# The last expert layer in pairs of slots with whole-batch rings, its loads and first gathers during the selection

## The chip, the cores and the metric

The kernel runs on one core of a Trainium2 chip. Time is device time in microseconds (us). The core's engines are TensorE (PE; its weight loads are shown as PEld), VectorE (DVE), ScalarE (ACT), GpSimd (POOL) and SyncE (SP). SyncE issues plain DMAs, GpSimd the indirect ones (gathers by an index per partition); 16 DMA engines carry both. Engines run their own instruction streams and meet at semaphores.

## The reference

x has the shape (8, 2048, 256) in float32: 8 batches of 2048 tokens. Three steps are added to it in turn:

```
x = x + 0.5 * ffn(layernorm(x));  x = x + attn(layernorm(x));  x = x + 0.5 * ffn(layernorm(x))
ffn(x):  gates  = sinkhorn(x @ gate_w)                  # (b, 2048, 8 experts), 8 iterations
         vals, idx = top_k(gates over the tokens, 256)  # per batch and expert
         out[e]    = x[idx[e]] @ experts[e] * vals[e]   # 256 tokens x 256, experts are 256 x 256
         result    = zeros(b, 2048, 256); result[idx] = out   # .set: of several experts on one token one wins
attn(x): a projection, a short convolution, a selective scan over 2048 steps with 16 states, a gate, a projection
```

## The kernel before

The program runs five stages, each with instruction streams of its own and a barrier of all engines behind it: constants; `route` "in" (gates and selection for the first ffn); `mixer` (the first ffn's experts and all of attn); `route` "mid" (L137 to L150: gates and selection for the second ffn); `ffn` (L1445 on: its experts and the final sum). The change is in the last two.

`route` has two halves. `gates_stage` loads all rows, normalises them, stores them to `normed_rows` in HBM and makes the gates. `top_stage` (L451 on) finds the 256 largest gates of each of 64 rows (batch, expert): VectorE does 32 rounds of MAX8, FIND_INDEX8 and MATCH_REPLACE8, merges two half rows by a bitonic exchange, and turns the result into tables. `slot_token` says for each slot of a batch which token it takes (a slot is 128 of the 256 places of one expert, so a batch has SL = 16 slots), `slot_gate` its gates, and `token_row`, which comes last, from which row of the results each token takes its own. For `token_row` VectorE builds 16 comparison tables (L603), which TensorE multiplies (L645).

`ffn` works by slots, and VectorE, GpSimd and SyncE have their streams unrolled over NB + 2 turns of a batch; TensorE and ScalarE do batch 0 written out and the others in a loop. For slot s of batch b:

- GpSimd gathers 128 tokens' rows into `f_picked` (L1532, "gather out"), after the turn of the slot 8 before;
- TensorE turns them (two transposes, L1606), one slot ahead of the products; VectorE copies the result from PSUM (L1570); TensorE multiplies by the expert's weights (L1613); ScalarE scales by the gate into `f_routed` (L1593); SyncE stores that to `routed_rows` (L1506).
- The way back: once all 16 stores of batch m have landed (and `token_row` is copied, L1562), GpSimd gathers for each of the 16 token tiles t the rows from `routed_rows` into `f_back` (L1544, "gather back"), VectorE adds them to `f_total`, which holds the batch's x (L1579), and SyncE stores the 2 MB when all 16 are added (L1513).

Every ring (`f_picked`, `f_routed`, `f_back`) has 8 buffers. The order is written out: in turn (b, s) GpSimd issues first the gather out of slot s and then the gather back that is BRING = 22 slots behind; VectorE does the copy of slot s and then the addition that is JOIN = 26 slots behind. So gather back t waits for the addition of t - 8, and that one stands in VectorE's order behind the copy of the slot four before the one that GpSimd is at:

```
pool.wait_ge(added, count(m * T + t - NK + 1))
```

The experts' 2 MB and the first two batches of x (2 MB each) are loaded by SyncE at the start of `ffn`; the loads of later batches go out between its stores.

Of the kernel before, what the change touches and what calls it, by code (L numbers as in the profile page):

```python
# [27 lines left out]
P = 128  # L28
NB = 8
# [9 lines left out]
YR = E * (M + 1)  # L39
ITERS = 8  # L40
# [96 lines left out]
def route(nc, g, x, tag):  # L137
# [3 lines left out]
    with ExitStack() as ctx:  # L141
        held = nc.snapshot_sems()
        rows = ctx.enter_context(nc.sbuf_tensor(f"gate_rows_{tag}", [P, NT // 2], F32))
        with ExitStack() as c1:
            gates_stage(nc, g, x_in, xn_out, rows, tag, c1)
        with ExitStack() as c1:
            top_stage(nc, g, rows, tag, c1)

        nc.clear_and_free_semaphores(nc.allocated_since(held))
        nc.all_engine_barrier()  # L150
# [300 lines left out]
def top_stage(nc, g, rows, tag, ctx):  # L451
# [40 lines left out]
    part_built, part_used, merged = sem("part_built"), sem("part_used"), sem("merged")  # L492
    ps_mirror = ctx.enter_context(nc.psum_tensor(f"ps_mirror_{tag}", [P, 2 * M], F32))
    FINAL = (M.bit_length() - 1) % 2
    block = ctx.enter_context(nc.Block())

    @block.gpsimd
    def _(pool):
        nc.gpsimd.memset(mirror[:], 0.0).then_inc(mirror_made, 1)
        pool.wait_ge(mirror_made, 1)  # L500
        nc.gpsimd.affine_select(out=mirror[:], in_=mirror[:], compare_op=ALU.not_equal, fill=1.0,
                                base=1 - P, pattern=[[1, P]], channel_multiplier=1).then_inc(mirror_made, 1)

    @block.vector
    def _(dve):
# [71 lines left out]
        def step(ins):  # L577
# [5 lines left out]
        dve.wait_ge(tok_copied, 1)  # L583
        flat = token_f[:].rearrange("p r h -> p (r h)")
# [5 lines left out]
        nc.vector.tensor_tensor(g.slot_token[:], token_f[:].rearrange("p (b e) h -> p b (e h)", b=NB),  # L590
                                g.token_base[:].unsqueeze(2).to_broadcast([P, NB, SL]), ALU.add)
# [853 lines left out]
def ffn(nc, g, x, out, ctx):  # L1445
# [11 lines left out]
    NX = NY = NK = 8  # L1457
    NT4 = 4
    BRING, JOIN, LOAD = SL + 6, SL + 10, 3
    expert = sb("f_expert", [P, E, KD, D])  # L1460
    slot_now = [sb(f"f_slot_now{i}", [P, SL], I32) for i in range(2)]
    row_now = [sb(f"f_row_now{i}", [P, T], I32) for i in range(2)]
    picked = [sb(f"f_picked{i}", [P, D]) for i in range(NX)]
    picked_t = [sb(f"f_picked_t{i}", [P, KD, P]) for i in range(NT4)]
    routed = [sb(f"f_routed{i}", [P, D]) for i in range(NY)]
    back = [sb(f"f_back{i}", [P, D]) for i in range(NK)]
    total = [sb(f"f_total{i}", [P, T, D]) for i in range(2)]
    ps_turn = [ps(f"f_ps_turn{i}") for i in range(NT4)]
    ps_out = [ps(f"f_ps_out{i}") for i in range(NT4)]
    expert_in, now_set, rows_set = sem("f_expert_in"), sem("f_now_set"), sem("f_rows_set")  # L1470
    picked_in = [sem(f"f_picked_in{i}") for i in range(NX)]
    routed_out = [sem(f"f_routed_out{i}") for i in range(NY)]
    back_in = [sem(f"f_back_in{i}") for i in range(NK)]
    x_in = [sem(f"f_x_in{i}") for i in range(2)]
    out_stored = [sem(f"f_out_stored{i}") for i in range(2)]
# [15 lines left out]
    def behind(b, s, lag):  # L1491

        k = (lag - s + SL - 1) // SL
        return b - k, s - lag + SL * k

    @block.sync
    def _(sp):
        def load_x(b):
            sp.dma_start(total[b % 2][:], x_v[b]).then_inc(x_in[b % 2], 16)

        def turn(b):
            for s in range(SL):
                e, h = s // NH, s % NH
                if there(b):
                    sp.wait_ge(scaled, b * SL + s + 1)
                    sp.dma_start(routed_v[b][e, 1 + h * P:1 + (h + 1) * P, :],  # L1506
                                 routed[s % NY][:]).then_inc(routed_out[s % NY], 16)
                if s == LOAD and there(b - 1) and there(b - 3):
                    sp.wait_ge(out_stored[(b - 1) % 2], (b - 1) // 2 * 16)
                    load_x(b - 1)  # L1510
                if s == JOIN - SL + 2 and there(b - 2):
                    sp.wait_ge(added, (b - 1) * T)
                    sp.dma_start(out_v[b - 2], total[b % 2][:]).then_inc(out_stored[b % 2], 16)  # L1513

        for e in range(E):
            sp.dma_start(expert[:, e, :, :], g.experts[e].rearrange("(k p) f -> p k f", p=P)).then_inc(expert_in, 16)
        load_x(0)
        load_x(1)
        rounds(turn)
        for odd in range(2):  # L1520
            sp.wait_ge(out_stored[odd], NB // 2 * 16)

    @block.gpsimd
    def _(pool):
        def turn(b):
            for s in range(SL):
                if there(b):
                    if s == 0:
                        pool.wait_ge(now_set, b + 1)
                    pool.wait_ge(turned, count(b * SL + s - NX + 1))  # L1530
                    pool.sem_inc(g.passed_pool, 1)
                    nc.gpsimd.indirect_dma_start(  # L1532
                        out=picked[s % NX][:], out_offset=None, in_=g.normed,
                        in_offset=bass.IndirectOffsetOnAxis(ap=slot_now[b % 2][:, s:s + 1].bitcast(U32), axis=0)
                    ).then_inc(picked_in[s % NX], 16)
                m, t = behind(b, s, BRING)
                if there(m):
                    if t == 0:
                        pool.wait_ge(rows_set, m + 1)
                        for k in range(NY):  # L1540
# [131 lines left out]
```

## Time and profile before

| | us |
|---|---|
| median of 3 runs (lowest, highest) | 3817.17 (3815.45, 3819.61) |
| the profiled execution | 3821.82 |
| its span, first to last instruction | 3820.3 |
| second selection (`top_stage` "mid") | about 3228 to 3413 |
| `ffn` | about 3413 to 3820 |
| mean granted TensorE clock | 0.856 |

A row of the timeline is: start, duration (us from the span's start), engine, line, operation, output<-inputs, sizes, count if alike instructions were merged, and in brackets the idle time of the engine before it and what ended it. "issue" means that the engine waited for nothing that the profile shows, "remote" that it waited for something that the profile can't name. An ending "q" (SPq) is an engine's queue: there the duration is from first to last issue. DMA-issuing instructions of GpSimd have durations of their own (DMA_INDIRECT); the data lands later. TensorE's ends are modelled. The clock is the granted share of full speed; its two levels are 0.5 (1.2 GHz) and 1.0 (2.4 GHz).

### The profile page before, as it was taken

The numbers are of one execution on the slowest core, as the hardware profiler recorded it, in microseconds if no ns is written. First come the engines' busy times: TensorE is split into PE (matmuls) and PEld (weight loads), VectorE is DVE, ScalarE is ACT, GpSimd is POOL, SyncE is SP. The second block draws the span as 40 slices with busy tenths as digits, with TensorE's granted clock in tenths as the row PEclk, the third lists the DMA queues.
The fourth block names the chain that finished last, engine by engine and source line by source line (L and its number), as shares of the span: only waits on it lengthen the run. The fifth ranks groups of instructions, "written<-read, shape, count | busy, mean of one in ns | idle before, by whom it ended". The sixth has DMA issues, their size and how long they took to land. (4 is left out here: it accounts for less than half of the span.)

```text
span 3820.3 us, 29742 instructions
## 1 busy us (share of the span) xinstructions
PE 2787.8 (73%) x9244; PEld 1524.3 (40%) x9244; DVE 3107.9 (81%) x2624; ACT 2135.3 (56%) x2286; POOL 1281.8 (34%) x900
## 2 busy tenths in 40 slices
PE   8701488899799889889989979997896695025553
PEld 4501233345345445434534634543442454014442
DVE  5798059999999999999999999989999467972222
ACT  6300366876876787688687687678766262001111
POOL 0000247245344443624624434440110100015665
PEclk9655799999999999999989999999998896557776
DMA  6200448778778868867877787886775471024666
GB/s 260 111 0 11 127 113 178 156 162 165 177 171 170 179 147 177 186 145 165 183 161 172 157 177 168 173 175 121 144 139 121 80 286 67 0 92 136 216 217 240
DMA packets 146762, 575.75 MB, mean 151 GB/s; under 512 B 22160, under 2 KB 73936, under 8 KB 99792
## 3 DMA queue, kind: packets, MB, share of 16 engines
q0 software_dynamic: 77568, 402.71, 50.9%
q1 hardware_dynamic: 69072, 171.59, 12.2%
q8 instruction: 55, 0.90, 0.1%
q14 instruction: 67, 0.55, 0.0%
HBM read 154.72 MB, written 117.51 MB: 71 GB/s over the span
## 5 line engine op out<-in xcount | busy, mean ns | idle before, releaser
L1057 DVE TENSOR_TENSOR_SCAN state<-state,drive 128x2048 f32<-128x2048 f32 x512 | 2220.8, 4405 | 75.7 <-ACT state L1222 75.7
L1222 ACT ACTIVATE state<-delta,neg_a 128x2048 f32<-128x2048 f32 x512 | 1020.2, 2003 | 276.1 <-DMA state<-state 186.2
L1393 PE MATMUL ps_states<-state,ident 128*128 128x512 f32 x1800 | 898.5, 646 | 167.6 <-DMA state<-state 167.6
L953 POOL DMA_DIRECT2D state<-state x256 | 232.8, 911 | 1288.9 <-DVE state L1057 1264.3
L1393 PEld LDWEIGHTS ps_states<-state,ident 128*128 128x128 f32 x1800 | 363.9, 209 | 608.4 <-issue 399.1
L1329 PE MATMUL ps_proj<-x1t,w_in 128*128 128x512 f32 x1024 | 502.5, 627 | 77.9 <-ACT conv_in L1138 59.2
L1345 PE MATMUL ps_proj<-conv_in,tap 128*128 128x512 f32 x1024 | 456.9, 594 | 0.5 <-ACT conv_in L1138 0.5
L901 POOL DMA_INDIRECT picked<-normed_rows,slot_now x128 | 368.7, 2880 | 256.0 <-DVE gate_now L995 188.8
L917 POOL DMA_INDIRECT x<-routed_rows,row_now x128 | 334.7, 2615 | 154.5 <-issue 64.3
L1329 PEld LDWEIGHTS ps_proj<-x1t,w_in 128*128 128x128 f32 x1024 | 196.1, 197 | 345.5 <-issue 235.8
L1345 PEld LDWEIGHTS ps_proj<-conv_in,tap 128*128 128x128 f32 x1024 | 191.7, 189 | 245.4 <-issue 244.7
L1570 DVE COPY f_picked_t<-f_ps_turn 128x256 f32<-128x256 f32 x128 | 54.0, 424 | 278.7 <-remote 140.3
L1613 PE MATMUL f_ps_out<-f_expert,f_picked_t 128*128 128x256 f32 x512 | 183.3, 495 | 97.6 <-DVE f_picked_t L1570 53.7
L1593 ACT ACTIVATE f_routed<-f_ps_out,slot_gate 128x256 f32<-128x256 f32 x128 | 60.5, 474 | 339.9 <-remote 139.5
L1361 PE MATMUL ps_rows<-w_out,xc 128*128 128x256 f32 x768 | 204.8, 391 | 5.0 <-DVE xc L1036 5.0
L1532 POOL DMA_INDIRECT f_picked<-normed_rows,f_slot_now x128 | 121.7, 951 | 229.4 <-DVE f_slot_now L1556 185.8
L1361 PEld LDWEIGHTS ps_rows<-w_out,xc 128*128 128x128 f32 x768 | 188.4, 306 | 19.2 <-issue 8.3
L1145 ACT COPY delta<-ps_proj 128x512 f32<-128x512 f32 x128 | 73.8, 582 | 177.4 <-PE ps_proj L1345 177.3
L1613 PEld LDWEIGHTS f_ps_out<-f_expert,f_picked_t 128*128 128x128 f32 x512 | 116.4, 251 | 123.5 <-DVE f_picked_t L1570 59.4
L1544 POOL DMA_INDIRECT f_back<-routed_rows,f_row_now x128 | 122.3, 955 | 108.6 <-issue 46.0
L1302 PE MATMUL ps_rows<-expert,picked_t 128*128 128x256 f32 x448 | 118.5, 388 | 17.5 <-ACT picked_t L1103 17.5
L1324 PE MATMUL ps_rows<-ident,x 128*128 128x128 f32 x256 | 46.2, 328 | 108.8 <-ACT x L1124 81.3
(267 smaller groups left out, 3177.1 us busy)
## 6 DMA issues: line engine op xcount, KB each, us to landing
state<-state POOLq DMA_DIRECT2D x256, 1024.0 KB, 7.7
delta<-xc POOLq DMA_DIRECT2D x24, 1024.0 KB, 12.3
normed_rows<-rows_in SPq DMA_DIRECT2D x8, 2048.0 KB, 7.5
expert<-in_experts SPq DMA_DIRECT2D x64, 256.0 KB
routed_rows<-routed SPq DMA_DIRECT2D x128, 128.0 KB
x<-in_x POOLq DMA_DIRECT2D x16, 1024.0 KB, 10.6
x_rows<-x SPq DMA_DIRECT2D x16, 1024.0 KB, 7.8
x_rows<-rows_out POOLq DMA_DIRECT2D x64, 256.0 KB, 8.6
```

The source lines that it names most:

```text
L901: nc.gpsimd.indirect_dma_start(out=picked[s % NX][:], out_offset=None, in_=g.normed, in_offset=bass.IndirectOffsetOnAxis(ap=slot_now[:, s: ...
L917: nc.gpsimd.indirect_dma_start(out=x1[:, t, :], out_offset=None, in_=g.routed[0], in_offset=bass.IndirectOffsetOnAxis(ap=row_now[:, t:t + ...
L953: nc.gpsimd.dma_start(out=state[held(q)][:], in_=state[held(q - 1)][:], accum_op=ALU.add).then_inc(pair_landed(b, q // 2)[0], 16)
L1057: nc.vector.tensor_tensor_scan(state[held(q)][:], state[held(q)][:], drive[j % 2][:], 0.0, ALU.mult, ALU.add).then_inc(state_ready, 1)
L1222: nc.scalar.activation(state[held(q)][:], delta[j % 2][:], ACT.Exp, scale=g.neg_a[:, j, n:n + 1]).then_inc(decay_ready, 1)
L1329: mm = nc.tensor.matmul(ps_proj[bank][:], g.w_in[:, k, col:col + P], x1t[:, k, c * CH:(c + 1) * CH], start=(k == 0), stop=(k == KD - 1))
L1345: mm = nc.tensor.matmul(ps_proj[c % 2][:], tap[:, j * KC + k, :], conv_in[:, c * CH + k:c * CH + k + CH], start=(k == 0), stop=(k == KC - 1))
L1361: mm = nc.tensor.matmul(out_bank(r, last)[:, (t % 2) * D:(t % 2 + 1) * D], y_now[j].rearrange("p (n t) -> p n t", t=T)[:, :, t], g.w_out[: ...
L1393: mm = nc.tensor.matmul(ps_sum[c][:], g.ident[:], state[held(q)][:, c * CH:(c + 1) * CH], start=(opening and n == 1), stop=(n == N - 1))
L1532: nc.gpsimd.indirect_dma_start(out=picked[s % NX][:], out_offset=None, in_=g.normed, in_offset=bass.IndirectOffsetOnAxis(ap=slot_now[b % 2 ...
L1544: nc.gpsimd.indirect_dma_start(out=back[t % NK][:], out_offset=None, in_=g.routed[m], in_offset=bass.IndirectOffsetOnAxis(ap=row_now[m % 2 ...
L1613: mm = nc.tensor.matmul(ps_out[s % NT4][:, 0:D], picked_t[s % NT4][:, k, :], expert[:, s // NH, k, :], start=(k == 0), stop=(k == KD - 1))
```

## The change

In `route` "mid", between the gates and the selection, the buffers of the last layer are laid out: the experts, six buffers of x (`f_total`, NTOTAL = 6, before: 2) and a ring of eight pairs of `f_picked`. During the selection SyncE loads the experts and six batches of x, and GpSimd issues the 16 gathers out of batch 0, as soon as `slot_token` is set; that addition is moved ahead of five small conversions.

In `ffn` all work on slots is by pairs (the two slots of one expert): one wait, one copy of 512 columns, one addition of 512 columns and one store of 256 KB for two; gathers, transposes, products and scalings stay as many as before. The rings of `f_picked`, `f_routed` and `f_back` hold 8 pairs, which is a whole batch. The gather back is BRING = 11 pairs (22 slots) behind as before, the addition JOIN = 13 pairs (26 slots). The order inside a turn is gather out x2, gather back x2. Batches 6 and 7 of x are loaded, and all outputs stored, in four pieces (PIECES) of 512 KB.

The diff, cut to its core:

```diff
+NTOTAL = 6
+PIECES = 4
 def route(nc, g, x, tag, ctx):
+    if tag == "mid":
+        g.f_expert = ctx.enter_context(nc.sbuf_tensor("f_expert", [P, E, KD, D], F32))
+        g.total = [... f"f_total{i}", [P, T, D] ... for i in range(NTOTAL)]
+        g.picked = [... f"f_picked{i}", [P, 2, D] ... for i in range(SL // 2)]
     with ExitStack() as c1:
         top_stage(nc, g, rows, tag, c1)
 def top_stage(nc, g, rows, tag, ctx):
+    @block.sync
+    def _(sp):
+        if tag == "mid":
+            for e in range(E):
+                sp.dma_start(g.f_expert[:, e, :, :], g.experts[e].rearrange(...)).then_inc(g.f_expert_in, 16)
+            for b in range(NTOTAL):
+                sp.dma_start(g.total[b][:], x_v[b]).then_inc(g.total_in[b], 16)
     @block.gpsimd
+        if tag == "mid":
+            pool.wait_ge(slots_set, 1)
+            for s in range(SL):
+                nc.gpsimd.indirect_dma_start(
+                    out=g.picked[s // 2][:, s % 2, :], out_offset=None, in_=g.normed,
+                    in_offset=bass.IndirectOffsetOnAxis(ap=g.slot_token[:, 0, s:s + 1].bitcast(U32), axis=0)
+                ).then_inc(g.picked_in[s // 2], 16)
     @block.vector
         dve.wait_ge(tok_copied, 1)
+        nc.vector.tensor_tensor(g.slot_token[:], token_f..., g.token_base..., ALU.add).then_inc(slots_set, 1)
         (five conversions)
-        nc.vector.tensor_tensor(g.slot_token[:], token_f..., g.token_base..., ALU.add)
 def ffn(nc, g, x, out, ctx):
-    NX = NY = NK = 8
-    BRING, JOIN, LOAD = SL + 6, SL + 10, 3
+    NP = SL // 2
+    NR = NP
+    BRING, JOIN = NP + 3, NP + 5
+    TP = T // PIECES
  SyncE:
+        def store_out(m, i):
+            sp.wait_ge(added, m * NP + (i + 1) * TP // 2)
+            sp.dma_start(out_v[m, :, i * TP:(i + 1) * TP, :], total[m % NTOTAL][...]).then_inc(out_stored[m % NTOTAL], 16)
+            for p in range(NP):
+                    sp.wait_ge(scaled, 2 * (b * NP + p + 1))
+                    sp.dma_start(routed_v[b][p, 1:1 + M, :].rearrange("(h q) d -> q h d", h=NH), routed[p][:])...
+                m, t = behind(b, p, JOIN + 3)
+                if there(m) and t % 2 == 0: store_out(m, t // 2)
+                old = b - 3
+                if p % 2 and there(old) and there(old + NTOTAL):
+                    sp.wait_ge(out_stored[old], PIECES * 16)
+                    load_x(old + NTOTAL, p // 2)
  GpSimd:
+            for p in range(NP):
+                if 1 <= b < NB:
+                    if p == 0: pool.wait_ge(now_set, b)
+                    pool.wait_ge(turned, count(b * NP + p - NR + 1))
+                    for h in range(2): (gather out of slot 2p + h)
+                m, t = behind(b, p, BRING)
+                if there(m):
+                    if t == 0:
+                        pool.wait_ge(rows_set, m + 1)
+                        for k in range(NR): pool.wait_ge(routed_out[k], (m + 1) * 16)
+                    pool.wait_ge(added, count(m * NP + t - NR + 1))
+                    for h in range(2): (gather back of tile 2t + h)
  VectorE:
+                    dve.wait_ge(turned, b * NP + p + 1)
+                    dve.wait_ge(product, count(b * NP + p - NT4 + 1))
+                    nc.vector.tensor_copy(picked_t[p % NT4][...], ps_turn[p % NT4][:]).then_inc(copied, 1)
+                    dve.wait_ge(back_in[t], (m + 1) * 32)
+                    nc.vector.tensor_tensor(total[m % NTOTAL][:, 2 * t:2 * t + 2, :], ..., back[t][:], ALU.add).then_inc(added, 1)
  TensorE: (4 transposes of pair p, then 8 matmul instructions of pair p - 1)
+            pe.wait_ge(picked_in[p], (b + 1) * 32)
+            pe.wait_ge(copied, b * NP + p + 1)
  ScalarE:
+                act.wait_ge(product, b * NP + p + 1)
+                act.wait_ge(routed_out[p], b * 16)
+                for h in range(2): (scale slot 2p + h)
```

## Rows read from the trace of the kernel before

**Rows 1.** Windows: length; busy of PE, PEld, DVE, ACT, POOL; clock; DMA share; GB/s.
```profile
3228.00:3413.00 185.00, 9.85 (x144) 7.44 (x144) 174.71 (x284) 0.62 (x2) 0.50 (x2) 0.50 0.00 0
...
3454.00:3785.00 331.00, 186.66 (x655) 137.96 (x653) 82.55 (x229) 52.08 (x111) 205.33 (x216) 0.72 0.61 196
```

**Rows 2.** Timeline of GpSimd in the last layer: gathers at its start and end.
```profile
3453.99 0.94 POOL L1544 DMA_INDIRECT f_back<-routed_rows,f_row_now  x1 [5.79 <-PE f_ps_turn L1606]
3455.24 0.94 POOL L1532 DMA_INDIRECT f_picked<-normed_rows,f_slot_now  x1 [0.30 <-issue]
...
3790.64 1.18 POOL L1544 DMA_INDIRECT f_back<-routed_rows,f_row_now  x1 [4.26 <-DVE f_total L1579]
...
3810.26 0.95 POOL L1544 DMA_INDIRECT f_back<-routed_rows,f_row_now  x1 [0.30 <-issue]
```

**Rows 3.** Waits of GpSimd, 3454 to 3785: total us, times, longest.
```profile
POOL f_back L1544 <- issue: 41.0, 83, 5.2
POOL f_back L1544 <- DVE f_total L1579: 40.0, 20, 5.1
```

**Rows 4.** Timeline of all engines, end of one stop in the last layer.
```profile
3529.60 0.47 ACT L1593 ACTIVATE f_routed<-f_ps_out,slot_gate 128x256 f32<-128x256 f32 x1 [6.81 <-remote]
...
3532.33 0.42 DVE L1570 COPY f_picked_t<-f_ps_turn 128x256 f32<-128x256 f32 x1 [8.49 <-remote]
...
3532.80 2.08 PE L1613 MATMUL f_ps_out<-f_expert,f_picked_t 128*128 128x256 f32 x4 [6.94 <-issue]
...
3533.87 0.94 POOL L1544 DMA_INDIRECT f_back<-routed_rows,f_row_now  x1 [3.29 <-remote]
```

**Rows 5.** Windows at the start of the last layer, columns as in rows 1.
```profile
3425.00:3429.00 4.00, 4.00 (x13) 3.07 (x14) 0.55 (x2) 0.52 (x2) 2.83 (x3) 0.53 1.01 416
3429.00:3437.00 8.00, 6.18 (x33) 4.59 (x32) 2.03 (x5) 2.70 (x6) 4.21 (x5) 1.00 1.00 398
```

**Rows 6.** Timeline of VectorE at the end of the second selection.
```profile
3384.22 0.29 DVE L590 TENSOR_TENSOR slot_token<-token_f_mid,token_base 128x128 int32<-128x128 f32 x1
3384.43 2.28 DVE L593 TENSOR_TENSOR at_tile_mid<-tile_f_mid,iota_col 128x2048 bf16<-128x2048 f32 x1
...
3389.07 18.25 DVE L603 TENSOR_TENSOR at_part_mid<-part_f_mid,iota_col 128x1024 bf16<-128x1024 f32 x16
...
3412.27 0.23 DVE L613 CAST token_row<-won_mid 128x128 int32<-128x128 f32 x1
```

**Rows 7.** Timeline of VectorE and GpSimd in the middle stage.
```profile
1036.75 17.36 DVE L1057 TENSOR_TENSOR_SCAN state<-state,drive 128x2048 f32<-128x2048 f32 x4
...
1043.75 2.60 POOL L901 DMA_INDIRECT picked<-normed_rows,slot_now  x1 [0.30 <-issue]
...
1051.58 3.41 POOL L901 DMA_INDIRECT picked<-normed_rows,slot_now  x1 [0.30 <-issue]
```

**Rows 8.** Instructions of line 901: durations in ns, minimum, median, maximum.
```profile
L901 POOL DMA_INDIRECT picked<-normed_rows,slot_now x128: 940/3402/4335, 375.1 to 2428.9; - x128
```

**Rows 9.** Timeline of TensorE in the last layer: its start, and two turns at full clock.
```profile
3421.34 0.69 PE L1606 MATMUL f_ps_turn<-ident,f_picked 128*128 128x128 f32 x2 [13.57 <-DMA f_picked<-normed_rows,f_slot_now]
...
3454.43 0.38 PE L1606 MATMUL f_ps_turn<-ident,f_picked 128*128 128x128 f32 x2
...
3455.52 0.38 PE L1606 MATMUL f_ps_turn<-ident,f_picked 128*128 128x128 f32 x2
```

**Rows 10.** Timeline: last slot of batch 5, gathered and scaled; last slot of batch 7, gathered.
```profile
3677.09 0.95 POOL L1532 DMA_INDIRECT f_picked<-normed_rows,f_slot_now  x1 [0.30 <-issue]
...
3692.49 0.47 ACT L1593 ACTIVATE f_routed<-f_ps_out,slot_gate 128x256 f32<-128x256 f32 x1 [4.57 <-remote]
...
3774.09 0.94 POOL L1532 DMA_INDIRECT f_picked<-normed_rows,f_slot_now  x1 [0.30 <-DVE f_total L1579]
```

**Rows 11.** Timeline: the last store.
```profile
3813.52 0.34 SPq L1513 DMA_DIRECT2D out<-f_total  x1
```

**Rows 12.** Waits of ScalarE over the last layer, 3413 to 3821.
```profile
ACT f_routed L1593 <- remote: 139.5, 31, 8.8
```

More of the change, by code:

```diff
@@ L1501, in turn @@
         def turn(b):
-            for s in range(SL):
-                e, h = s // NH, s % NH
+            for p in range(NP):
                 if there(b):
[L1505 to L1518, printed above, removed]
+                    sp.wait_ge(scaled, 2 * (b * NP + p + 1))
+                    sp.dma_start(routed_v[b][p, 1:1 + M, :].rearrange("(h q) d -> q h d", h=NH),
+                                 routed[p ][:]).then_inc(routed_out[p ], 16)
+                m, t = behind(b, p, JOIN + 3)
+                if there(m) and t % 2 == 0:
+                    store_out(m, t // 2)
@@ L1597, in _, with turn @@
+        pairs(0)
         with act.Fori(1, NB) as b:
[L1598 removed]
+            pairs(b)
     @block.tensor
     def _(pe):
[L1602 to L1604 removed]
+        def turn(b, p):
+            pe.wait_ge(picked_in[p], (b + 1) * 32)
+            pe.wait_ge(copied, count(b * NP + p - NT4 + 1))
             for k in range(KD):
[L1606 removed]
+                for h in range(2):
+                    c = k * 2 + h
+                    mm = nc.tensor.transpose(ps_turn[p % NT4][:, c * P:(c + 1) * P], picked[p ][:, h, k * P:(k + 1) * P],
+                                             g.ident[:])
@@ L1607, in turn @@
             mm.then_inc(turned, 1)
-        def apply_expert(b, s):
-            pe.wait_ge(copied, b * SL + s + 1)
-            pe.wait_ge(scaled, count(b * SL + s - NT4 + 1))
-            for k in range(KD):
-                mm = nc.tensor.matmul(ps_out[s % NT4][:, 0:D], picked_t[s % NT4][:, k, :], expert[:, s // NH, k, :],
-                                      start=(k == 0), stop=(k == KD - 1))
-            mm.then_inc(product, 1)
-        def slots(b):
-            for s in range(SL + 1):
-                if s < SL:
-                    turn(b, s)
-                if s == 1 and isinstance(b, int):
-                    pe.wait_ge(expert_in, E * 16)
-                if s:
-                    apply_expert(b, s - 1)
@@ L1626, in _, with apply_expert, pairs @@
-        slots(0)
+        def apply_expert(b, p):
+            pe.wait_ge(copied, b * NP + p + 1)
+            pe.wait_ge(scaled, count(2 * (b * NP + p - NT4 + 1)))
+            for h in range(2):
+                for k in range(KD):
+                    mm = nc.tensor.matmul(ps_out[p % NT4][:, h * D:(h + 1) * D], picked_t[p % NT4][:, k, h, :], expert[:, p, k, :],
+                                          start=(k == 0), stop=(k == KD - 1))
+            mm.then_inc(product, 1)
+        def pairs(b):
+            for p in range(NP + 1):
+                if p < NP:
+                    turn(b, p)
+                if p == 1 and isinstance(b, int):
+                    pe.wait_ge(g.f_expert_in, E * 16)
+                if p:
+                    apply_expert(b, p - 1)
@@ L1627, in _ @@
+        pairs(0)
         with pe.Fori(1, NB) as b:
-            slots(b)
+            pairs(b)
 def program(nc, w, g):
```

155 lines of the change are left out of this document (75 added, 80 removed).

## The prediction, before the run

> **What bounds the kernel now.** I read stage windows first, then GpSimd's waits, then the order in time of the last stage. The windows show a second selection (3228 to 3413 us) in which VectorE is busy 174.7 of 185 us, GpSimd 0.5 us and the DMA share is 0.00, and then the last expert layer, in which no engine is full: from 3454 to 3785 TensorE is busy 187 of 331 us at a granted clock of 0.72, VectorE 83, ScalarE 52, GpSimd 205, DMA 0.61 [rows 1]. What the layer does throughout is issue gathers on GpSimd, 256 of them. One takes 0.94 us, and the next starts 1.25 us after it where nothing holds it (3453.99, 3455.24) [rows 2]. From the first gather back (3453.99) to the last (3810.26) there are 232 steps in 356.3 us; at 1.25 us they would be 290.0, so 66.3 us are stalls. The waits name them: gathers back wait 40.0 us for additions (20 times, up to 5.1 us) and 41.0 us with no releaser shown (83 times, the ordinary 0.30 us gaps among them) [rows 3]. The reader should see the rhythm behind it: after about seven gathers out and seven back, GpSimd stops for 3 to 5 us, because the gather into ring buffer t needs the addition of t-8, and that addition stands on VectorE behind a copy that waits for TensorE. At 3529.60 ScalarE ends a wait of 6.81 us, at 3532.33 VectorE one of 8.49 us, both for "remote", and at 3533.87 GpSimd goes on [rows 4]. TensorE's results reach the others late when TensorE has caught up with the gathers; a ring of 8 is too short to bridge that.
>
> So three things are to be had: the stalls (66 us), the start of the layer (3413 to 3454 us, where batch 0 is computed and no gather back may go), and the end (10.0 us from the last gather's start to the span's end).
>
> **The change, part by part.** All against this execution (3821.8 us, span 3820.3; the median of the runs is 4.6 us less, and I carry the difference over unchanged).
>
> (a) *Loads moved into the selection.* Eight expert loads and six batches of rows, some 14.6 MB, go out from SyncE at the selection's start, where DMA idles for 185 us and SyncE has nothing else. 14.6 MB at the 400 GB/s of 3421 to 3429 us [rows 5] are 37 us. Nothing queues behind. Cost 0; bound above: if these writes slowed VectorE by 1%, 2 us. They also leave the layer's start, where they held DMA at 1.00 until 3437 [rows 5] and delayed the first gathers.
>
> (b) *Sixteen gathers moved into the selection.* They follow the addition that makes the token numbers, now ahead of five small casts: about 3383.3 instead of 3384.22 [rows 6]. Issued freely they would be done 16 x 1.25 = 20 us later, well before the selection's end at 3412.5. But VectorE then runs operations with two SBUF inputs: two of 2.28 (one is shown) and 16 whose pitch is 18.25/16 = 1.14 us [rows 6]. In the middle stage such a neighbour holds a gather: beside the scans one took 2.60 and 3.41 us, and the median of 128 is 3.40 [rows 7, 8]. 1043.75+2.60 = 1046.35 is 0.93 us behind a scan boundary (1036.75 plus two scans of 4.34 is 1045.43): the gather waits for VectorE's next boundary and then takes its usual time. With a pitch of 1.14 and a need of 0.95+0.30 = 1.25 it misses every second boundary, so one gather per 2.27 us. Two or three go by 3389, eight until 3407.3, five or six more at 1.25: the last ends at 3414.5, 2 us behind VectorE, and the barrier waits for GpSimd. Cost +2 us (bounds: 0, if nothing holds them; +6, at 3.4 us each until 3407 and 1.25 after). Four scans with a gather ending among them took 17.36 us, 4.34 each [rows 7], so VectorE itself loses nothing. The Trainium skill ("SBUF — State Buffer", on the shared port pair) says that a VectorE operation with two SBUF inputs and a GpSimd operation that reads SBUF exclude each other for a whole instruction, whichever starts first. By that VectorE could be held 0.95 us per gather, some +10 us more; the scans' unchanged pitch speaks against it.
>
> (c) *Start of the layer.* Before, TensorE began at 3421.34 [rows 9], behind the first gather, and was granted the full clock at about 3428.8 (0.53 on average over 3425 to 3429, 1.00 after) [rows 5]. Now it begins at 3413.6+2+0.4 = 3416.0 with all 16 gathers landed. For 7.5 us at half clock it does a slot in about 2.2 us (2.08 for the products alone; estimated with the turn's share), 3.5 slots; the other 12.5 at full clock take 1.09 each (3454.43 to 3455.52) [rows 4, 9]: 3416.0+7.5+13.6 = 3437.1. Scaling 2 x 0.47, store and landing about 3.8 with GpSimd's start: first gather back at 3441.8 instead of 3454.0. **-12.2 us**, (b) included. GpSimd issues four pairs meanwhile and idles; it has 232 gathers left, against 233.
>
> (d) *Rings of a batch.* A gather out waits for the turn eight pairs earlier; a gather back for an addition whose copy is due six pairs, 30 us, earlier, against four slots, 10 us, now. The late results (up to 8.5 us) fit into that. The 231 steps then take 288.8 us. Pairing saves no issue time: the 0.30 us gap stays (lower bound 0, at best 0.1 us x 116). What is late next is the wait for the batch's last store, by the first gather back of a batch. Between the last gather out of a batch and that one there are now 16 others, so 17 x 1.25 = 21.3 us. Today's chain for a last slot: gather at 3677.09, scaled at 3692.49 [rows 10], plus about 3 to land: 18.4; at the end 3774.09 to 3790.64 [rows 2, 10], 16.6. A pair adds one product and one copy, 3 us at half clock. 18 to 21: just covered. I take 1 us for each of six batches and 2 for gathers that DMA slows: **+8** (bounds 0 and +35, when each batch loses 5). TensorE needs 16 x 2.2 = 35 us a batch at half clock and 40 are there.
> At the last batch only 8 gathers stand between: 11.3 us against a chain of about 16: +5, about what it costs now.
> Last issue: 3441.8+288.8+8+5 = 3743.6.
>
> (e) *Tail.* The last store is 512 KB rather than 2 MB. 2 MB went out at 3813.52 and ended the span, 6.8 us [rows 11]. I keep an estimated 1.8 fixed and a quarter of the rest: 3.0. With landing 2.8, a double addition 0.7 and 0.8 around them, 7.3 instead of 10.0: **-2.7** (bounds 0, -5). Copies, additions and stores in pairs (half the instructions on VectorE and SyncE) lie beside GpSimd's pace: 0, and nothing even if that cover went, as both are mostly idle.
>
> Sum: span 3743.6+7.3 = 3750.9 against 3820.3, **-69.4 us**; median 3817.2-69.4 = 3747.8, say 3748.
>
> **Rivals.** *R1, TensorE's late results keep the pace.* If after each catch-up the handshake turn, copy, product costs 7 to 9 us whatever the rings, the deeper ring only moves the queue. For: the waits for "remote" are not named by any queue, and ScalarE alone has 139.5 us of them [rows 12]; TensorE looks only one pair ahead. Against: slots whose gathers are there run at 1.1 to 2.2 us, so a backlog is worked off faster than GpSimd makes it. Then a third to all of the 66 us stay: 3770 to 3805, middle 3787.
> *R2, it ends slower.* The first gather back of each batch waits for the last pair's store. Every late result in that chain adds to GpSimd's path; to eat 69 us over seven batches it must cost 10 us each, a chain beyond 31 us. The longest seen is 18.4 [rows 10]; two late results of 8.5 us and a pair at half clock would give 32: 3820 to 3830.
> *R3, the gathers in the selection hold VectorE*, by the lock above: 16 x 0.95 = 15 us on top, and TensorE waits for the tables: 3763.
> *R4, no effect*: only if GpSimd's stalls are replaced one for one and the start gains nothing; the start's 12 us speak against it: 3810 to 3824.
>
> **How the numbers follow.** Forecast as it stands (3733 to 3768, with R3) 0.66; R1 0.25; R4 0.04; R2 0.05. The forecast's floor is no stall at all and a free start: 3748-8-5-2 = 3733. The range 3732 to 3800 leaves out the top of R1, R2 and R4. This kernel's measurement tells 0.2% (8 us) from nothing: faster by more 0.92, within 0.03, slower 0.05.
>
> **What would show it.** Right: 16 gathers in the selection at about 2.3 us pitch, ending some 2 us behind VectorE; TensorE's first transpose within 1 us of the barrier; first gather back near 3442; then GpSimd at 1.25 us with no stop every seventh pair, and additions gone from its waits; last gather near 3744. Wrong: GpSimd waiting for stores or turns by several us in each batch (R1, R2: pitch over 1.35 us), VectorE's 16 comparisons longer than 18.3 us (R3), or TensorE's clock so low that its slots pass 2.5 us.

## The result: 0.7 per cent slower, and the profile after

The changed kernel took 3846.91 us (median, 3843.97 to 3847.82) beside 3816.31 (3810.79 to 3819.61) for the kernel before: ratio 1.0071, 95% interval 1.0058 to 1.0084. The forecast was 3748. Its profiled execution has a span of 3845.3 us (before 3820.3).

Waits of GpSimd in the last layer from the first gather back on (total us, times, longest); they answer to [rows 3]:

```profile
POOL f_back L1568 <- DMA routed_rows<-f_routed: 85.4, 6, 17.0
POOL f_back L1568 <- issue: 51.8, 117, 16.5
...
POOL f_back L1568 <- DVE f_total L1603: 14.4, 3, 13.8
```

The stops every seven pairs are gone, as forecast. In their place stands one stop per batch of up to 17.0 us, at the first gather back, which waits for the stores of the batch to land. (Of the seven, 16.51 and 13.76 us stand in the other two rows; the first row has 12.45 us of batch 0 as well, which was forecast.) The reader should see where it starts. Timeline of batch 3's late part, some lines left out (start, duration, what, idle time of its engine before it and what ended that):

```profile
3566.41 0.95 POOL L1568 DMA_INDIRECT f_back<-routed_rows,f_row_now  x1 [0.30 <-issue]
3566.44 1.89 PE L1643 MATMUL f_ps_out<-f_expert,f_picked_t 128*128 128x256 f32 x8
...
3568.17 0.60 PE L1634 MATMUL f_ps_turn<-ident,f_picked 128*128 128x128 f32 x4
...
3590.12 0.94 POOL L1555 DMA_INDIRECT f_picked<-normed_rows,f_slot_now  x1 [0.30 <-issue]
3595.07 0.84 ACT L1618 ACTIVATE f_routed<-f_ps_out,slot_gate 128x256 f32<-128x256 f32 x2 [27.87 <-remote]
...
3596.41 0.69 DVE L1594 COPY f_picked_t<-f_ps_turn 128x512 f32<-128x512 f32 x1 [18.97 <-remote]
...
3607.03 1.26 POOL L1568 DMA_INDIRECT f_back<-routed_rows,f_row_now  x1 [15.96 <-DMA routed_rows<-f_routed]
```

The product that TensorE's records end at 3568.3 is scaled at 3595.07, 26.7 us later; the turn recorded until 3568.8 is copied at 3596.41, 27.6 us later. ScalarE had stood idle for 27.87 us by then and VectorE for 18.97. From 3566.41 to 3590.12 GpSimd issued a gather every 1.25 us. A single result came through meanwhile (the copy at 3576.07, itself 9.5 us late); these two, and with them everything that waited, came only within 6 us of the end of its last gather (3591.1). I call this a **hold**: a result of TensorE that is finished by its records and that the others see late. The readers are not what is slow: the times at which TensorE's semaphores rose are in the trace too, 3594.95 us for this product and 3596.39 for this turn, 0.12 and 0.02 us ahead of the two that waited for them. So the semaphore rises late. Whether TensorE's execution is late as well, the records don't tell; they do have its next turn begun at 3580.11, in the middle of the hold. The pattern is regular: from the first gather back on, GpSimd starts again seven times after such a long stop while TensorE has work left. Each time the first result that is late ends on TensorE 12.2 to 15.5 us after that start, and the last one is seen 3.9 to 5.6 us after GpSimd's next stop.

Lateness is counted from the recorded end on TensorE to the start of the instruction that uses the result. Added up over all turns and products that are over 1.5 us late, the holds are 605 us in 37 results, the longest 27.6, against 451 us in 92 results, the longest 13.5, before. These times overlap each other. Counted only from when the engine that uses the result was free, they are 383 us (longest 26.7) against 298 (8.5). There too they end behind GpSimd's stops: at [rows 4], 3529.60 and 3532.33 us. With a ring of eight slots GpSimd ran dry after seven pairs and so ended each hold early; with rings of a batch it can run on until the batch ends.

The parts that were forecast well, in one timeline (TensorE's first turn, the gathers that open the layer, the last gather and store) and VectorE's comparisons in the selection, which answer to [rows 2, 6, 9, 11]:

```profile
3389.73 18.26 DVE L624 TENSOR_TENSOR at_part_mid<-part_f_mid,iota_col 128x1024 bf16<-128x1024 f32 x16
...
3412.97 0.99 POOL L520 DMA_INDIRECT f_picked<-normed_rows,slot_token  x1 [0.30 <-issue]
3417.72 1.94 PE L1634 MATMUL f_ps_turn<-ident,f_picked 128*128 128x128 f32 x8 [9.30 <-PEq L155]
3443.44 0.94 POOL L1568 DMA_INDIRECT f_back<-routed_rows,f_row_now  x1 [12.45 <-DMA routed_rows<-f_routed]
...
3837.27 0.95 POOL L1568 DMA_INDIRECT f_back<-routed_rows,f_row_now  x1 [0.30 <-issue]
3837.10 5.12 SPq L1524 DMA_DIRECT2D out<-f_total  x2
```

By the prediction's terms: 3443.4 (3441.8 forecast) + 288.8 + 105.0 of stalls (13) + 8.0 (7.3) = 3845.3. The 105.0 us are the first gathers back of batches 1 to 6 (88.8), that of batch 7 (12.3) and gathers that took longer than 0.95 us (4.0), each rounded.

### The profile page after: what moved, and what is told of

Its sections match the earlier page's. It is cut to its first block and busy times, and to the rows that moved or that the text cites. A ratio compares the mean times of both kernels' runs of the same rounds, so it can differ in the third digit from the quotient of the medians.

```text
span 3845.3 us, 29066 instructions
## 1 busy us (share of the span) xinstructions
PE 2774.3 (72%) x9244; PEld 1521.5 (40%) x9244; DVE 3092.4 (80%) x2495; ACT 2127.6 (55%) x2286; POOL 1293.2 (34%) x900
## 5 line engine op out<-in xcount | busy, mean ns | idle before, releaser
L1594 DVE COPY f_picked_t<-f_ps_turn 128x512 f32<-128x512 f32 x64 | 44.1, 690 | 322.7 <-remote 212.2
L1643 PE MATMUL f_ps_out<-f_expert,f_picked_t 128*128 128x256 f32 x512 | 160.8, 472 | 146.7 <-DVE f_picked_t L1594 118.5
L1555 POOL DMA_INDIRECT f_picked<-normed_rows,f_slot_now x112 | 108.2, 966 | 41.1 <-issue 32.6
## 6 DMA issues: line engine op xcount, KB each, us to landing
delta<-xc POOLq DMA_DIRECT2D x24, 1024.0 KB, 12.3
```

Source lines behind the costliest of these rows:

```text
L1643: mm = nc.tensor.matmul(ps_out[p % NT4][:, h * D:(h + 1) * D], picked_t[p % NT4][:, k, h, :], expert[:, p, k, :], start=(k == 0), stop=(k ...
```

## The experiments

Theories: **T1**, GpSimd's gathers, issued back to back, hold TensorE's results, and the hold ends when GpSimd stops; **T2**, TensorE's idleness or low clock does it, whatever GpSimd does; **T3**, the waits for register values in the loops of TensorE and ScalarE. The runs added a fact that none of them had: some chips have no holds. The table names the chip of each run. "Holds" is the sum of late results as counted above; "pause" is a GpSimd memset ahead of each pair of gathers, with its length in us.

| run | chip | this, us | before beside it | ratio (95%) | holds, us (longest) |
|---|---|---|---|---|---|
| e1 four ahead | 14 | 3749.8 | 3757.9 | 0.9976 (0.9966 to 0.9985) | 0 |
| e2 unrolled | 14 | 3748.8 | 3757.9 | 0.9976 (0.9966 to 0.9985) | 0 |
| e3 fill | 14 | 3760.4 | 3757.9 | 1.0007 (0.9997 to 1.0016) | 0 |
| e4 before, rings of 16 | 14 | 3755.9 | 3757.9 | 0.9996 (0.9986 to 1.0005) | 0 |
| e5 changed | 12 | 3839.2 | 3818.1 | 1.0056 (1.0038 to 1.0075) | 613 (27.7) |
| e6 before | 12 | 3818.4 | 3818.1 | 0.9998 (0.9988 to 1.0007) | 503 (11.8) |
| e7 four ahead | 3 | 3797.7 | 3810.6 | 0.9958 (0.9943 to 0.9973) | 312 (14.4) |
| e8 fill | 3 | 3884.7 | 3810.6 | 1.0182 (1.0158 to 1.0207) | 679 (31.4) |
| e9 unrolled | 3 | 3835.0 | 3810.6 | 1.0062 (1.0043 to 1.0081) | 563 (27.2) |
| e10 pause 0.76 | 4 | 3813.0 | 3811.6 | 1.0004 (0.9995 to 1.0014) | 0 |
| e11 pause 0.22 | 4 | 3835.6 | 3811.6 | 1.0061 (1.0044 to 1.0078) | 493 (25.6) |
| e12 narrow rows | 4 | 3836.9 | 3811.6 | 1.0073 (1.0056 to 1.0089) | 647 (27.6) |
| e13 pause 0.43 | 10 | 3779.9 | 3758.0 | 1.0057 (1.0040 to 1.0073) | 0 |
| e14 pause 0.57 | 10 | 3791.5 | 3758.0 | 1.0088 (1.0068 to 1.0107) | 0 |
| e15 pause and four | 10 | 3768.1 | 3758.0 | 1.0025 (1.0016 to 1.0035) | 0 |
| e16 before, pauses | 10 | 3832.4 | 3758.0 | 1.0193 (1.0176 to 1.0211) | 0 |
| e17 pause 0.43 | 10 | 3777.8 | 3761.7 | 1.0058 (1.0038 to 1.0078) | 0 |
| e18 changed | 10 | 3749.0 | 3761.7 | 0.9969 (0.9959 to 0.9979) | 0 |

**First four: e1 to e4.** GpSimd at most four pairs ahead:

```diff
-                    pool.wait_ge(turned, count(b * NP + p - NR + 1))
+                    pool.wait_ge(turned, count(b * NP + p - 4 + 1))
-                    pool.wait_ge(added, count(m * NP + t - NR + 1))
+                    pool.wait_ge(added, count(m * NP + t - 4 + 1))
```

> Edit: the changed kernel, with its sixteen buffers, but GpSimd may be no more than four pairs of gathers ahead of the turned pairs and of the added pairs (it was eight). Theory T1 (gathers issued back to back hold back what TensorE has finished; the hold ends only when GpSimd stops): GpSimd stops every four to seven pairs again as in the kernel before, no result is later than about 14 us (27.6 in the changed kernel), the sum of late results over 1.5 us falls from 605 us to below 450 although each stands for a pair, the wait at each batch's first gather back goes from 14-17 us to under 6, and the time is 3785 to 3815. Theory T2 (TensorE idles and its clock falls, whatever GpSimd does): the same late results, 20 us and more, and now GpSimd waits for them as well: 3850 to 3890. Theory T3 (register waits in the loops of TensorE and ScalarE): as T2.

Loops written out (TensorE and ScalarE):

```diff
-        pairs(0)
-        with pe.Fori(1, NB) as b:
-            pairs(b)
+        for b in range(NB):
+            pairs(b)
```

> Edit: the changed kernel with the loops of TensorE and ScalarE over batches 1 to 7 written out, so that each wait is for a constant. T3: late results go away (sum below 100 us instead of 605), time 3745 to 3765, what was forecast. T1 and T2: nothing changes, 3840 to 3852, results up to 25 us late as before.

More work on TensorE (the wait for the experts, moved ahead of the first turn, is left out here):

```diff
-            pe.wait_ge(picked_in[p], (b + 1) * 32)
             pe.wait_ge(copied, count(b * NP + p - NT4 + 1))
+            for _ in range(2):
+                nc.tensor.matmul(ps_turn[p % NT4][:], g.ident[:], expert[:, p, :, :].rearrange("p k d -> p (k d)"),
+                                 start=True, stop=True)
+            pe.wait_ge(picked_in[p], (b + 1) * 32)
```

> Edit: in the last layer TensorE does two more matmuls of 512 columns on each pair, into the turn's bank before the turn, ahead of its wait for the gather; their result is written over. That is 2 x 0.86 = 1.7 us of added TensorE work per pair at full clock, 3.4 at half, in a pitch of 5.0 us. T2 (it is TensorE's idleness or its low clock that lets results come late): late results nearly vanish, granted clock over 0.95 in the layer, GpSimd never stops for long, 3745 to 3765. T1 in its plain form (the gathers alone do it): results stay 20 us late and the longer work adds: 3845 to 3900. A mixed form (both needed) reads as T2 here, and as T1 in the run with four pairs.

The kernel before with larger rings alone:

```diff
-    NX = NY = NK = 8
+    NX = NY = NK = 16
```

> Edit: the kernel before with rings of sixteen single slots instead of eight in its last layer, nothing else: no pairs, no early gathers. T1: GpSimd runs on for longer, so results are held for longer than the 13.5 us at most before, up to 20 us and more, GpSimd's stops are fewer and longer, and the layer gains nothing or loses: 3810 to 3850 (before: 3816). If pairs are the cause (a pair's result is one increment, and both banks wait for it), the larger rings alone take away stops: 3750 to 3800. T2: no result is later than before, 3790 to 3816.

Measured: all four had no hold at all, and the kernel before took 3757.9 us beside them, 58 less than known. So e1 to e3 told T1, T2 and T3 apart in nothing: what each would have removed wasn't there. Read alone, e2 would have looked like a proof of T3. Only the time of the kernel before warns of that. e4 does say something: where there are no holds, rings of 16 slots instead of 8 are worth 0.9996 (0.9986 to 1.0005), nothing that the measurement can tell. Its GpSimd has no wait longer than the ordinary 0.30 us between 3454 and 3720 us; two of the rows:

```profile
POOL f_back L1544 <- issue: 28.6, 94, 0.3
POOL f_picked L1532 <- issue: 26.5, 87, 0.3
```

**Controls: e5, e6.** Both kernels unedited.

> The changed kernel itself, once more. In the four runs before this one no result of TensorE was late (none over 1.5 us, against 605 us of them in the changed kernel's first profile), whatever was edited, and the kernel before took 3758 us beside them instead of 3816. Theory C (the holds belong to the chip or to its state, not to the edits): where the kernel before takes about 3758 us, this one has no holds and takes 3745 to 3752, 0.1 to 0.4 per cent under it; where the kernel before takes about 3816 us, it has the holds of up to 27 us again and takes 3840 to 3850. Theory E (the edits took the holds away): it is slower than the kernel before on any chip, ratio 1.005 to 1.009.

> The kernel before itself, for its profile on the same chip. Theory C: if it takes about 3758 us its profile shows no late result and no stops of GpSimd in the last layer apart from the start and the end, so that rings of eight slots cost nothing there; if it takes about 3816 us, late results of up to 14 us and a stop of 3 to 5 us in every seven or so pairs of gathers. Theory E: stops and late results as in its first profile on any chip.

Measured: chip 12 has the holds, 613 us of late results in the changed kernel and 503 in the kernel before (11.8 at most). The time of the changed kernel, 3839.2 us, lies 1 us under theory C's range. That the holds belong to the chip or its state (theory C) is what all runs bear out: they are there on chips 12, 3 and 4, wherever the kernel before takes 3811 to 3818 us (the first result, whose chip isn't on record, belongs here with 3816), and not on 14 and 10, where it takes 3758 to 3762. No run told why.

One more difference goes with the chips, and it makes a rival that no run tested. A trace has a record of every rise of a DMA's semaphore, 16 for each DMA. For the changed kernel there are 20,088 of them in e18, where nothing is held, but 15,907 in its first trace and 15,999 in e5, and some nine tenths of those that are missing belong to the last layer. Between 3440 and 3740 us e18 has 5138 records for 324 DMAs, the first trace 1108 for 246. So on a chip with holds most of these records are lost while results are held; e10 further down, without a late result on such a chip, has 3552 for 265. It may be the recording itself that holds TensorE's semaphores, when gathers make more records than such a chip can take away. All times here are of executions with a span and a clock on record, so none tells whether the holds are there without any recording.

**The same edits with holds: e7 to e9** (chip 3).

> GpSimd no more than four pairs ahead, once more, for a chip on which the holds are there (the kernel before at about 3816 us beside it). T1 (gathers issued back to back hold TensorE's finished results back, and the hold ends when GpSimd stops): stops every four to seven pairs, no result over 14 us late, sum of late results under 450 us (605 and 613 in the changed kernel), 3785 to 3825. T2 (TensorE idle or at its low clock, whatever GpSimd does) and T3 (register waits): results 20 us late remain, 3840 to 3890. If the kernel before takes 3758 us beside it, it says nothing new: 3745 to 3753 again.

T1 foretold it, T2 and T3 did not: 312 us of late results, 14.4 at most (T1 had said 14), 3797.7 us, 0.9958. GpSimd's waits in e7 are short again, as in the kernel before, and for additions, instead of one long one per batch:

```profile
POOL f_back L1568 <- DVE f_total L1603: 48.0, 11, 5.7
...
POOL f_back L1568 <- DMA routed_rows<-f_routed: 3.3, 1, 3.3
```

> Two more matmuls of 512 columns per pair on TensorE ahead of its wait for the gather, once more, for a chip with the holds. T2 or a mixed form (it takes an idle TensorE for the gathers to hold it back): late results nearly gone, sum under 100 us, 3755 to 3775, that is as on the chip without holds (3760). T1 in its plain form: results 20 us late, 3845 to 3900.

T2 fell. Timeline of e8 in batch 2 (GpSimd went on at 3512.57 after a stop of 19.42 us):

```profile
3520.39 1.89 PE L1646 MATMUL f_ps_out<-f_expert,f_picked_t 128*128 128x256 f32 x8
...
3522.12 1.88 PE L1631 MATMUL f_ps_turn<-f_expert,ident 128*128 128x512 f32 x4
...
3523.84 0.60 PE L1637 MATMUL f_ps_turn<-ident,f_picked 128*128 128x128 f32 x4
...
3524.05 0.84 ACT L1618 ACTIVATE f_routed<-f_ps_out,slot_gate 128x256 f32<-128x256 f32 x2 [4.67 <-remote]
...
3524.28 1.89 PE L1646 MATMUL f_ps_out<-f_expert,f_picked_t 128*128 128x256 f32 x8
...
3526.01 1.88 PE L1631 MATMUL f_ps_turn<-f_expert,ident 128*128 128x512 f32 x4
...
3540.20 0.84 ACT L1618 ACTIVATE f_routed<-f_ps_out,slot_gate 128x256 f32<-128x256 f32 x2 [15.31 <-remote]
```

By its records TensorE works without a gap from before 3512 until 3528.3, at a granted clock of 1.00, and still the product that ends at 3522.3 is scaled 1.8 us late and the next (3526.2) 14.0 us late. So the hold takes neither an idle TensorE nor its low clock. It sets in 10 us after GpSimd resumed; over e8's seven such starts it is 8.1 to 10.8 us, sooner than the 12.2 to 15.5 of the changed kernel. The time, 3884.7 us, is T1's plain form, 3845 to 3900.

> The loops of TensorE and ScalarE written out, once more, for a chip with the holds. T3 (register waits): holds gone, 3745 to 3755. T1 and T2: as the changed kernel, 3835 to 3850, sum of late results 550 to 650 us.

T3 fell: 563 us of late results and 3835.0 us without any loop.

**The rate: e10 to e12** (chip 4). Ahead of each pair of gathers in the last layer (768 columns; 128 in e11):

```diff
+                    pool.wait_ge(idled, n_idle[0])
+                    n_idle[0] += 1
+                    nc.gpsimd.memset(idle[:], 0.0).then_inc(idled, 1)
                     for h in range(2):
```

> Edit: the changed kernel, with a GpSimd memset of 768 columns (about 1.1 us by the 0.19 us of one of 128 columns) ahead of each pair of gathers in the last layer, so that gathers go two at a time with 1.1 us between pairs (120 pauses, 132 us in all). T1r (it takes gathers at about one in 1.25 us; with pauses between them TensorE's results come through): no result over 3 us late, no stops, time = 3750 + 132 less what stops cost = 3860 to 3885 on any chip. T1s (it takes a stop of some us, short pauses don't help): results 20 us late remain, 3900 to 3980 on a chip with holds.

The memset took 0.76 us and not 1.1, a pair of gathers 3.12 instead of 2.50. Timeline of GpSimd in e10:

```profile
3600.46 0.76 POOL L1557 MEMSET f_idle<- 128x768 f32 x1
3601.39 1.46 POOL L1559 DMA_INDIRECT f_picked<-normed_rows,f_slot_now  x1 [0.17 <-issue]
3603.16 0.95 POOL L1559 DMA_INDIRECT f_picked<-normed_rows,f_slot_now  x1 [0.30 <-issue]
3604.10 0.75 POOL L1573 MEMSET f_idle<- 128x768 f32 x1
3605.01 0.95 POOL L1575 DMA_INDIRECT f_back<-routed_rows,f_row_now  x1 [0.16 <-issue]
```

Not one result was over 1.5 us late on a chip that has holds (e11 and e12, on the same chip, have them), and from 3445 us on no wait of GpSimd was over 2.3 us. This is T1r: the rate counts, and no long stop is needed. The time of 3813.0 lies under the 3860 to 3885 expected, because the pauses were shorter: 120 of them at 0.63 us are 75 us, and it is 64 over the 3749.0 of the changed kernel where there are no holds (e18). So even these pauses cost less than the holds (e11 and e12 beside it: 3836 and 3837).

> Edit: as the run with 1.1 us, with a memset of 128 columns, 0.2 us, ahead of each pair of gathers (24 us in all, if it doesn't fit beside a gather's 0.3 us of gap). T1r with a threshold just under the present rate: holds gone, 3760 to 3780, better than the kernel before on a chip with holds. T1s, or a threshold far off: sum of late results still above 450 us, 3845 to 3875.

Here a pair took 2.59 us where nothing else held it, one gather per 1.29 us, and the holds were nearly whole: 493 us. The time of 3835.6 is under the 3845 to 3875 expected for that. Between one gather per 1.29 us and one per 1.56 us lies the rate at which they begin.

The rows back cut to 32 of 256 columns (the sum is not the reference's):

```diff
-   out=back[t ][:, h, :], out_offset=None, in_=g.routed[m],
+   out=back[t ][:, h, 0:32], out_offset=None, in_=g.routed[m].rearrange("r (q c) -> (r q) c", c=32),
```

> Edit: the gathers back take rows of 32 columns instead of 256 (and the adds add 32 columns), from a view of the table with an eighth of the row; so the sum isn't the reference's. GpSimd issues as many gathers of 128 rows as before, while half of them move an eighth of the bytes. If the holds come from the bytes that gathers move or from the DMA engines' load: results at most 10 us late, sum under 300 us, 3750 to 3800. If they come from GpSimd's issuing of gathers itself: as the changed kernel, sum 550 to 650 us, 3830 to 3850.

Windows of 3454 to 3800 us, of the changed kernel, then of e12, then of e10 (length; PE, PEld, DVE, ACT, POOL busy; clock; DMA share; GB/s):

```profile
3454.00:3800.00 346.00, 153.37 (x606) 120.50 (x604) 63.43 (x110) 41.70 (x100) 195.40 (x204) 0.72 0.51 160
```

```profile
3454.00:3800.00 346.00, 150.77 (x595) 117.96 (x596) 41.95 (x115) 41.99 (x100) 191.72 (x203) 0.70 0.42 126
```

```profile
3454.00:3800.00 346.00, 182.70 (x615) 139.31 (x614) 71.90 (x122) 43.67 (x104) 293.63 (x324) 0.72 0.57 177
```

e12 moves 34 GB/s less than the changed kernel and has 647 us of holds. By itself that leaves room, as only a fifth of the bytes are gone, and the averages hold the stops too. But e10, on the same chip, moves 177 GB/s on average and 197 to 201 in each 20 us from 3540 to 3600, without a hold; e12 moves 193 to 223 in the 12 to 15 us before a hold sets in and 129 to 137 over the whole of such a run of gathers. So the bytes don't tell a held run from a free one. What does is the rate at which gathers are issued, or something that goes with each gather or descriptor: their semaphores, or the records of them.

**The last six: e13 to e18** (chip 10, without holds).

> Edit: a memset of 384 columns (0.43 us by the 0.22 of 128 and 0.76 of 768 columns) ahead of each pair of gathers while gathers out are still issued, none in the last eight pairs back; one gather per 1.40 us. The 119 pauses of 0.63 us made about 57 us over the 3756 without stops, so these make some 25. Rate theory with the threshold under 1.40 us: no result late, no stops, 3775 to 3790 (before about 3812 beside it). Threshold over 1.40: late results of 10 to 20 us remain, 3820 to 3850.

> Edit: as the run with 384 columns, with 544 columns, 0.57 us, one gather per 1.47 us. No late results, 3785 to 3800, some 12 us over the run with 384 if that has no holds either; if that one has them and this has none, the threshold lies between.

> Edit: both cures: memset of 256 columns (0.33 us, one gather per 1.35 us) and GpSimd no more than four pairs ahead. If holds grow rarer step by step with the rate: late results below half of the 312 us of the run with four pairs alone, 3780 to 3795. If 1.35 us is as bad as 1.25: the same late results and the pauses on top, 3800 to 3815.

> Edit: the kernel before, with a memset of 768 columns ahead of each gather out, that is one pause of 0.63 us per two gathers, one gather per 1.56 us as in the run with pauses of 0.63 us. Rate theory: late results and GpSimd's stops of 3 to 5 us vanish here too, though the ring has eight slots; so the ring cost nothing by itself. The pauses add 128 x 0.63 = 80 us less what lies under the tail, stops give back about 55: 3820 to 3845. If the stops come from the ring of eight: they stay, 3870 to 3895.

> Pauses of 0.43 us ahead of each pair of gathers, one gather per 1.40 us, once more. On a chip with holds (the kernel before at about 3812 us): threshold under 1.40 us: no late results, 3780 to 3792, 0.6 per cent under the kernel before; threshold over 1.40: late results of 10 to 20 us, 3820 to 3850. On a chip without holds 3776 to 3784 again.

e13, e14, e15 and e17 are e10 with 384, 544, 256 (and four ahead) and 384 columns, none while only gathers back are left. They met no holds, so they give prices alone: 31, 43, 19 and 29 us over the 3749 of the changed kernel there. e16 (one pause per gather out in the kernel before) lost 74 us; that its 3832.4 lies in the range of the rate theory is chance, as this chip has no holds for the pauses to take away. Where between 1.29 and 1.56 us the holds begin, whether a pause of 0.43 us would pay on a chip with them, and whether the pauses would also empty the kernel before of its stops, stays open.

> The changed kernel itself. On a chip without holds (the kernel before at about 3758 us): no late result, 3745 to 3752, ratio 0.997 to 0.999: the earlier first gather back (12 us less, of which the start of the rings of the kernel before gives up no more) and nothing from its rings. On a chip with holds: 3834 to 3850, ratio 1.0056 to 1.008, as in its two profiles so far.

This one hit: 3749.0 us, 0.9969 (0.9959 to 0.9979), no late result. Its timeline of GpSimd (first gather back, the wait of the last batch, the last gather):

```profile
3440.95 0.95 POOL L1568 DMA_INDIRECT f_back<-routed_rows,f_row_now  x1 [10.98 <-DMA routed_rows<-f_routed]
...
3723.03 0.95 POOL L1568 DMA_INDIRECT f_back<-routed_rows,f_row_now  x1 [5.58 <-DVE f_total L1603]
...
3742.28 0.95 POOL L1568 DMA_INDIRECT f_back<-routed_rows,f_row_now  x1 [0.30 <-issue]
```

3441.0 + 288.8 + 12.5 + 7.5 = 3749.8, beside the forecast's 3441.8 + 288.8 + 13 + 7.3 = 3750.9. The 12.5 are made up otherwise than the 13: nothing for the first gathers back of batches 1 to 6 (6 forecast), 5.3 for the last batch (5), and 6.6 for 25 gathers that took longer than 0.95 us (2).

**A version for both kinds of chip.** The changed kernel with GpSimd four pairs ahead (e7 and e1) is a little faster than the kernel before on both kinds of chip: 0.9958 with holds and 0.9976 without. The changed kernel is slower on the first (1.0056 to 1.0071) and no different from this version on the second (0.9969; the intervals overlap).

## Why the prediction was wrong

It failed at **step (d)**, the rings of a batch, in the sentence "The late results (up to 8.5 us) fit into that", and with it in the cover of 21.3 us for the chain behind a batch's last gather out. With longer rings the results came up to 27.6 us late, and the chain took 34.7 to 38.0 us.

- What bounds the kernel: the rhythm was read rightly, stops of 3 to 5 us with late results just ahead of their end. The reading of it was the wrong way round. "A ring of 8 is too short to bridge that" takes the lateness as given and the ring as what suffers; the stop was what ended the lateness. With the ring longer, the longest lateness grew from 13.5 to 27.6 us; with GpSimd kept to four pairs (e7) it was 14.4. The 66.3 us of stalls [rows 3] were no reserve of the rings. Where there are no holds, the kernel before takes as long as e4 (0.9996), whose GpSimd has no such stops; that it has none there either is concluded from that, as it was not profiled on such a chip. With holds, longer rings put the short stops together into long ones.
- (d), the last store: the chain from a batch's last gather out until its results have landed was put at 18 to 21 us from [rows 10], just under the cover of 21.3. In batches 1 to 6 it measured 31.6 to 34.9 us to the scaled result, for instance 3570.2 to 3603.4 in batch 3, and 34.7 to 38.0 to the first gather back, which stopped for 13.6 to 17.0 us for it. 105.0 us of stalls instead of 13: that is 92 of the 94.4 us of error. Rows 10 were also no upper bound: batch 1 of the kernel before took 16.7 us to the scaled result, so some 20 with the landing, and not 18.4.
- (a) and (b) were right. The gathers beside the comparisons came one per 2.27 us, the last in the selection ended at 3413.96 (3414.5 forecast), and VectorE's 16 comparisons took 18.26 us beside them, 18.25 before [rows 6]. So VectorE was not held, and what the Trainium skill ("SBUF — State Buffer", on the shared port pair) would have made of it, 0.95 us for each gather, didn't show.
- (c) was right to 1.6 us (3443.4), with TensorE's first turn at 3417.72 instead of 3416.0. (e) was right to 0.7 (8.0); its fixed 1.8 us of a store stood on no row, and the last store of 512 KB, issued after the addition that ended at 3841.87, took about 3.4 us to the span's end, against 3.0.
- Rivals: R2 is what happened, chain beyond 31 us and all. It was given a chance of 0.05 and 10 us per batch, because its lateness was capped at the longest seen before; its 3820 to 3830 still lay 17 us under the measured time. R1 had the late results keep the pace but for a part of the old 66 us, never for more. R3 and R4 are out.

On a chip without holds the time is 1 us from the forecast (3749.0 against 3748). That is in part luck: the parts of (d) came out otherwise than forecast and their sum alone was right (12.5 against 13). And the gain there is 13 us (8 to 9 by e1 and e2) and not 69, as the kernel before starts from 3758 to 3762 us and not from 3816.

## What to carry to other kernels

A stall in a rhythm may be what ends the trouble that it seems to come from. Ask what stops while it lasts, before giving the engine that stops a longer ring. When an engine waits for "remote" and the work it waits for has long ended in the records, don't cap the lateness at the longest one seen. Run the kernel before beside each experiment and look at its time first: the first four, on a chip that hadn't the trouble, would have "proved" whatever theory they were to test. And look at what a trace has lost, not only at what it shows.

## What the runs showed of the hardware

- On chips 12, 3 and 4, and not on 14 and 10, results of TensorE reached the others up to 31.4 us after their recorded end (e8) while GpSimd issued indirect DMAs of 128 rows at one per 1.25 us. In the changed kernel's first trace this set in 12.2 to 15.5 us after GpSimd began, in e8 8.1 to 10.8, and in both it ended within 6 us of GpSimd's last gather. It is the rise of TensorE's semaphore that is late: 29 of the 30 late results of the first trace whose reader stood idle have it on record, 0.02 us (VectorE) or 0.12 us (ScalarE) before the reader begins. Results of ScalarE and VectorE showed nothing of the kind: the scaling of 3595.07, 0.84 us long, had its store issued at 3595.93, and the copy of 3596.41, 0.69 long, its product begun at 3597.24.
- One gather per 1.56 us (e10, 197 to 201 GB/s for 60 us): none late; one per 1.29 us (e11): 493 us of late results. Rows of 128 bytes instead of 1 KB on every second pair (e12, 193 to 223 GB/s before a hold) left 647 us of them.
- Traces with late results have lost most records of DMA semaphores in the last layer (1108 left for 246 DMAs between 3440 and 3740 us, of 16 each; without holds 5138 for 324). Whether the recording causes the lateness was not tested.
- The kernel before took 49 to 60 us more on chips with holds (3811 to 3818) than on those without (3758 to 3762). What tells such chips apart, and whether it is the chip or a state of it, no run showed.
